# Dense attention's quotients stored, its finish loaded by chunks and joined with the norm, and idle matmuls at the head of eight stages

## The reference

```python
xn = _layernorm(x, ln_gamma, ln_beta)
q = (xn @ w_q).reshape(B, SQ, NUM_HEADS, DIM_HEAD)        # 16 heads of 64
k, v = jnp.split(context @ w_kv, 2, axis=-1)              # 1601 keys
attn = softmax(einsum('bqhd,bkhd->bhqk', q * SCALE, k))
out = einsum('bhqk,bkhd->bqhd', attn, v).reshape(B, SQ, INNER)   # INNER = 1024
return (out @ w_out + b_out) * tanh(gate[0])
...
x = _layernorm(x + _L1_xattn_ref(x, ...))
x = _layernorm(x + _L1_ffn_ref(x, ...))
```

## Time and profile before

| | us |
|---|---|
| median of three executions (lowest, highest) | 8678.82 (8678.73, 8685.87) |
| the profiled execution, whole | 8695.39 |
| the profiled execution, span of the trace | 8693.6 |
| busy in the span: PE, DVE, ACT, POOL | 6502.8, 6476.1, 4444.7, 3965.1 |
| dense attention `l1xc`, from the window's row | 6933 to 8447 |
| its finish and the norm behind it | 8447 to 8622 |

### The profile page before, as it was taken

One profiled execution on the slowest core, in us unless ns is written; L12 is line 12 of the kernel. 1 busy time (PEld: TensorE's weight loads), 2 busy tenths in 40 slices (PEclk: granted clock), 3 DMA queues, 4 the chain that ended last, 5 costly groups with the idle time before them and its releaser, 6 DMA issues. The chain is left out here.

```text
span 8693.6 us, 157925 instructions
## 1 busy us (share of the span) xinstructions
PE 6502.8 (75%) x31114; PEld 2666.4 (31%) x31240; DVE 6476.1 (74%) x41675; ACT 4444.7 (51%) x8491; POOL 3965.1 (46%) x2643
## 2 busy tenths in 40 slices
PE   6998477774677767998566777776657899999974
PEld 3333222221222224665222232222223322222213
DVE  4664899999999994554799999999996444444424
ACT  1665466664666652112567777776655332323320
POOL 0001355553555541221456666665644065656650
PEclk7999666665666667999677777776767999999986
DMA  2000000000000000000000000000000411111122
GB/s 75 19 22 12 31 8 5 8 5 4 8 5 8 8 2 17 22 15 16 32 9 5 7 8 9 6 9 5 6 5 19 164 31 31 38 40 31 31 47 64
DMA packets 81575, 193.10 MB, mean 22 GB/s; under 512 B 23728, under 2 KB 38062, under 8 KB 77230
## 3 DMA queue, kind: packets, MB, share of 16 engines
q1 hardware_dynamic: 72366, 169.98, 7.0%
q10 hardware_dynamic: 8192, 12.59, 0.6%
HBM read 118.97 MB, written 62.76 MB: 21 GB/s over the span
## 5 line engine op out<-in xcount | busy, mean ns | idle before, releaser
L2152 DVE TENSOR_REDUCE l1xc_part_max<-l1xc_by_query 128x1 f32<-128x512 f32 (+1 forms) x1024 | 559.5, 571 | 753.3 <-PE l1xc_by_query L2011 731.4
L2110 ACT ACTIVATE l1xc_prob<-l1xc_less_max 128x512 f32<-128x512 f32 (+1 forms) x832 | 451.2, 594 | 1004.4 <-PE l1xc_less_max L2025 935.9
L582 PE MATMUL l1ac_by_query<-l1ac_k_stack,l1ac_q_stack 97*128 (+1 forms) x1024 | 423.0, 470 | 695.8 <-ACT keep_xT L677 364.2
L770 DVE MAX8 l1ac_cand<-l1ac_score 128x8 f32<-128x39 f32 (+1 forms) x6656 | 863.1, 192 | 31.8 <-ACT l1ac_score L677 17.0
L552 POOL TENSOR_SCALAR l1ac_lost<-l1ac_score,l1ac_tops 128x2048 bf16<-128x2048 f32 x128 | 696.0, 5437 | 411.4 <-DVE l1ac_tops L789 387.1
L582 PE MATMUL l0xc_by_query<-l0xc_k_stack,l0xc_q_stack 97*128 (+2 forms) x1024 | 375.1, 431 | 664.8 <-ACT keep_xT L677 448.7
L770 DVE MAX8 l1ac_cand<-keep_xT 128x8 f32<-128x39 f32 (+1 forms) x6656 | 863.0, 191 | 4.4
L1973 POOL TENSOR_TENSOR l1xc_total<-l1xc_total,l1xc_prob 128x2048 f32<-128x2048 f32 (+1 forms) x176 | 794.2, 4513 | 72.3 <-POOL l1xc_v_tile L1983 72.0
L770 DVE MAX8 l0xc_cand<-l0xc_score 128x8 f32<-128x31 f32 (+1 forms) x6656 | 800.9, 182 | 27.6 <-ACT l0xc_score L677 15.8
L552 POOL TENSOR_SCALAR l1ac_lost<-keep_xT,l1ac_tops 128x2048 bf16<-128x2048 f32 x128 | 696.3, 5440 | 244.4 <-DVE l1ac_tops L789 244.4
L770 DVE MAX8 l0xc_cand<-keep_xT 128x8 f32<-128x31 f32 (+1 forms) x6656 | 801.7, 182 | 4.4
(11 more groups left out here) (479 smaller groups left out, 14320.9 us busy)
## 6 DMA issues: line engine op xcount, KB each, us to landing
l1xc_k<-wide_k SPq DMA_DIRECT2D x32, 400.2 KB
moe_w<-in_L_ffn_mlp_w_dram SPq DMA_DIRECT2D x16, 512.0 KB, 4.2
wide_q<-l1xp_full SPq DMA_DIRECT2D x8, 1024.0 KB, 3.9
wide_q_parts<-l1xp_parts SPq DMA_DIRECT2D x16, 512.0 KB, 5.5
l1xc_q_hm<-wide_q_parts SPq DMA_DIRECT2D x32, 256.0 KB, 3.8
l1xc_q<-wide_q SPq DMA_DIRECT2D x32, 256.0 KB
wide_sums<-l1xc_o_out ACTq DMA_DIRECT2D x64, 128.0 KB, 2.3
l1xf_num<-wide_sums SPq DMA_DIRECT2D x16, 512.0 KB, 11.6
```

The source lines that it names most:

```text
L582: nc.tensor.matmul(sA[c % 2][:, 0:w], Qm[0:SHIFT_ROW, bass.ds(at + i * P, P)], Kb[0:SHIFT_ROW, bass.ds(at + a, w)], start=True, stop=True) ...
L770: seg = nc.vector.max(new[:, j:8 * NSEG:NSEG], score[i % 4][:, a:a + w])
L2110: nc.scalar.activation(prob[0:n, buf(j), c], yP[c % 2][0:n], ACT.Exp).then_inc(y_taken, 1)
L2152: nc.vector.tensor_reduce(part_max[:, i % 2, c:c + 1], a_bank(i, c)[:, 0:w], AX.X, ALU.max).then_inc(a_taken, 1)
```

## The change

Six things are edited.

1. **Quotients are stored.** `denominators` runs in two halves, p = 0 at the end of tile j = 0 and p = 1 at the end of j = 1, each of two matmuls with ones of 64 columns; the second waits until DVE has emptied the bank. DVE takes two reciprocals (128x512 each) into a new tile `inv`, at the start of j = 1 and of j = 2. POOL multiplies `o_out` by them (`divide`, at the end of its j = 2 and j = 3). ACT's `store` moves from j = 2 to j = 4 and issues four DMAs where it issued eight.
2. **The finish's loads begin early.** SP loads `w_out` into the free `ctxT`, and the rows of the first four heads into `xT`, at the end of `attend_wide`. The other six chunks are loaded in `finish_wide` by groups of 512 queries (three DMAs of 512 KB each), with a semaphore for each group.
3. **No wait for all eight.** PE begins with a group's four tiles once its three loads have landed. DVE's eight multiplies are gone. The bias is added to x by POOL, times tanh(gate), as `finish_rows` does, so PE's matmul for it is gone.
4. **The norm is joined.** Statistics, roots and scalings follow tile by tile inside `finish_wide`, as in `finish_rows`; the block `l1xm` is gone. The transposes into `xT` stay.
5. **Idle matmuls** (`idle`, the same as L918): 14 ahead of each `project`, 20 ahead of each `layer_norm` but the last, 24 ahead of the gate's loads and 30 behind its logits, 28 ahead of `finish_wide`.
6. `wide_sums` has the shape (1024, 2048).

```diff
+def idle(nc, G, bank, n):
+    for _ in range(n):
+        nc.tensor.matmul(bank[:], G.identb[:], G.zerob[:], start=True, stop=True)
...
         @block.tensor                                   # project
         def _(pe):
+            idle(nc, G, banks[3], 14)
             pe.wait_ge(loaded, 6 * 16)
...
         @block.tensor                                   # layer_norm
         def _(pe):
+            if out is None:
+                idle(nc, G, banks[1], 20)
             if affine:
 
                 pe.wait_ge(loaded, 32)
...
         @block.tensor                                   # moe_gate
         def _(pe):
+            idle(nc, G, banks[2], 24)
             pe.wait_ge(loaded, LOADS)
...
             mm.then_inc(logged, 1)
+            idle(nc, G, banks[2], 30)
             pe.wait_ge(weighed, 1)
...
             stats(H - 1)                                # attend_wide, SP
+            w_out = G.ctxT[:].rearrange("p c n -> p (c n)")[:, 0:XC * D]
+            sp.dma_start(w_out.rearrange("p (c n) -> p c n", c=XC),
+                         A["L1_xattn_w_out"].rearrange("(c p) n -> p c n", p=P)).then_inc(fetched, 16)
+            sp.wait_ge(o_stored, 64 * 2 * KC + 16)
+            for c in range(KC):
+                sp.dma_start(G.xT[:, c], G.wide_sums[c * P:(c + 1) * P, :]).then_inc(fetched, 16)
+            sp.wait_ge(fetched, 16 * (KC + 1))
...
-                    hold(pool, (o_formed, h + 1))
+                    hold(pool, (o_formed, 2 * h + 2))
...
+            def divide(h, p):
+
+                hold(pool, (inverted, 2 * h + 3 + p), (o_taken, 2 * h + 4))
+                nc.gpsimd.tensor_tensor(O_out[:, p], O_out[:, p], inv[:, p], ALU.mult).then_inc(o_ready, 1)
...
-                for c in range(QC):
-                    mm = nc.tensor.matmul(Den[32 * c:32 * (c + 1), :], G.ones[:, 0:32], total[:, c],
+                hold(pe, (inverted, 2 * h + 2 + p))
+                if p == 0:
+                    hold(pe, (added_p, ADDS * (h + 2)), (st_out, h + 2 if last else h + 3))
+                for r in range(2):
+                    mm = nc.tensor.matmul(Den[r * XH:(r + 1) * XH, :], G.ones[:, 0:XH], total[:, 2 * p + r],
                                           start=True, stop=True, skip_group_check=True)
...
         @block.tensor                                   # finish_wide
         def _(pe):
-            pe.wait_ge(normed, XC)
+            def out(t):
+                if t % 4 == 0:
+                    pe.wait_ge(loaded[t // 4], 16 * EARLY // 2)
...
+            idle(nc, G, banks[3], 28)
+            pe.wait_ge(row_loaded, 32)
...
+            for t in range(QT):
+                out(t)
+                if t >= 6 and t % 4 == 2:
+                    turn_back(t // 4 - 1)
+            turn_back(G4 - 1)
```

More of the change, by code:

```diff
@@ L915, in turn_back @@
                     mm.then_inc(back_turned, 1)
-            for _ in range(IDLE):
-                nc.tensor.matmul(banks[3][:], G.identb[:], G.zerob[:], start=True, stop=True)
+            idle(nc, G, banks[3], 14)
             weights()
@@ L1995, in _ @@
             add(H - 1, NKT - 1)
+            for p in range(2):
+                divide(H - 1, p)
         @block.tensor
@@ L2074, in head @@
                             by_query(ha, 1 - slot, i, c)
-                    if j == 0 and not first:
-                        denominators(hb - 1)
+                    if j < 2 and not first:
+                        denominators(hb - 1, j)
             def a_end(h):
@@ L2238, in _ @@
-            nc.tensor.matmul(gate_bank[:, 0:1], G.ones[0:1, 0:P], gate[:], start=True, stop=True).then_inc(gated, 1)
-            pe.wait_ge(normed, XC)
-            for t in range(QT):
+            def out(t):
+                if t % 4 == 0:
+                    pe.wait_ge(loaded[t // 4], 16 * EARLY // 2)
                 if t >= 4:
@@ L2248, in _ @@
+            idle(nc, G, banks[3], 28)
+            pe.wait_ge(row_loaded, 32)
+            nc.tensor.matmul(row_bank[:, 0:D], G.ones[0:1, 0:P], bias[:], start=True, stop=True)
+            nc.tensor.matmul(row_bank[:, D:D + 1], G.ones[0:1, 0:P], gate[:], start=True, stop=True).then_inc(spread_formed, 1)
+            for t in range(QT):
+                out(t)
+                if t >= 6 and t % 4 == 2:
+                    turn_back(t // 4 - 1)
+            turn_back(G4 - 1)
         @block.scalar
```

158 lines of the change are left out of this document (100 added, 58 removed).

## The result

| us | before | after |
|---|---|---|
| median of the first comparison | 8682.35 (4 executions) | 8585.59 (4) |
| the traced execution | 8695.39 | 8583.69 |
| median of all executions of this study | 8685.7 (44; 8674.6 to 8708.3) | 8583.7 (8; 8571.5 to 8586.7) |

The ratio of the first comparison is 0.9886, 95% interval 0.9869 to 0.9903: faster by 1.1%. The forecast was 8554, range 8532 to 8577. So the direction was right and the forecast gain too large: 124.8 us forecast, 111.7 between the two traced executions, 102 between the medians of all.

The account below looks back on a forecast made before the run. Loads bound the finish's first part, PE its second, a DVE-ACT-DVE-PE chain its third; PE's waits count in the attention. -94.5 - 21 - 9.3 = -124.8, taken from the median 8678.82, gives 8554 us, range 8532 to 8577.

Parts of the forecast that it names:

- The finish: Final block of the dense attention: early loads and joined norm bring the next block 94.5 us earlier.
- The last quotients: Between attention and finish: two halves of sums, two reciprocals, a multiply and four issues end the block 2.8 us later.
- The load rate of 205 GB/s: Finish's first loads: 1.5 MB at the old rate take 7.3 us, so PE may start 9.3 us in.
- The attention: Dense attention: removing PE's waits on ACT saves 15.8 us over 14 heads and 5.2 in head 15, together 21.
- PE's four matmuls for `den` stay four.: Sums over the keys in each head: splitting them in two halves keeps four matmuls; reciprocals item taken as 0 us.
- The forecast's rival at 8575: Dense attention: a bank wait behind the reciprocals, 1.1 us a head, gives back the 21 us; chance 11%.
- The clock at the jumps: Loop jumps in the dense attention: clock falls, 20.6 us before, change by 0 in the middle, 12 either way.
- The stages are the same in the median run: Whole kernel: the gain against the traced 8695.39 us was also subtracted from the median 8678.82, giving 8554.
- The idle rows: Idle matmuls ahead of projections and norms and in the gate: gains and costs sum to -9.3 us.
- The gate: Idle matmuls there delay the chain by 3.2 to 4.2 us and save 1.5: net +2.2, bounds 0 and +4.
- the idle rows give nothing: Rival for the idle matmuls: 11.5 us of gains go, 3.7 of cost stay, about 8566; chance 14%.
- the list of what would show it: Trace signs named beforehand for right or wrong: waits on ACT, multiply times, first tile, tile spacing, gate's square, head lengths.

Follow-up runs that it names:

- e1: The kernel before the change, run once more unchanged: 8685.8 us, ratio 0.9994; its traced execution took 8696.4.
- e8: The changed kernel run again unedited, on the same chip as some of its variants: 8581.0 us, ratio 0.9884; its traced execution took 8571.5.
- e2: The changed kernel with one pass of sums a head (four 32-column matmuls), both reciprocals kept, output not the reference's: 8555.9 us, ratio 0.9845.
- e3: The changed kernel without any idle matmuls except the finish's 28: 8582.6 us, ratio 0.9877.
- e11: The changed kernel without the finish's 28 idle matmuls: 8581.7 us, ratio 0.9881; finish block 73.9 us against 73.2.
- e12: The changed kernel with each of the finish's twelve loads cut into two halves of 64 partitions: 8581.4 us, ratio 0.9887; finish block 75.0 us.
- e4: The changed kernel without the 24 idle matmuls at the head of the gate: 8577.4 us, ratio 0.9869; gate 71.7 us.
- e10: The changed kernel without the gate's 24 idle matmuls, and with 22 instead of 14 ahead of `l1ap`: 8581.3 us, ratio 0.9886; `l1ap` 80.6 us.
- e6: The changed kernel with four heads in one turn of the dense attention's loop, two jumps back instead of six: 8564.2 us, ratio 0.986.
- e7: The changed kernel with each of a head's four store DMAs cut into two of 32 rows, eight issues: 8582.7 us, ratio 0.9884.

## Why the prediction was wrong, step by step

The forecast was 29.7 us under the changed kernel's 8583.7 (the median of all its executions, and its first traced one). Of these 13.1 are terms of the sum, 9.7 the traced execution that the sum was made against (8695.4 over a median of 8685.7), and 6.9 the base: three executions gave 8678.8 where 44 give 8685.7. The 13.1 are good to some 13 us, since the traces of e1 and e8 differ by the full 124.9; so the steps below rest on stages and heads, and on e2 and e3, rather than on that sum.

- **The finish: right**, -96.9 for -94.5 (with e8's trace -94.5). The last quotients cost 2.0 more, 1.4 of it by the same step that failed in the attention: half of the sums was priced at half the time. The prediction's own sum is also some 0.4 short there: with its five hand-overs its terms end at 8451.0, not 8450.6. The block was 4.3 shorter: tiles 3.45 and not 3.65, since without the matmul of the bias between two tiles the eight take 0.2 less (3.2 in all), the start 0.4 and the tail 0.6 earlier. The load rate of 205 GB/s was wrong (388), but the idle row held the start: it ended 8.2 us in, and without it PE waited for the loads until 7.7 (e11). At 233 GB/s it would have been worth a wait of 1.0 (e12).
- **The attention: the failing step is "PE's four matmuls for `den` stay four."** Their time was taken as a time per instruction. It is a time per pass over the array's columns: four times 32 and twice 64 both take 1.06 to 1.08. e2 takes the second pass away and nothing else: PE's busy time in a head falls from 89.59 to 88.67 us and the head from 91.6 to 90.7. Rebuilt without chance: waits on ACT -15.8, last head -5.3 (72.6 to 67.3; -5.2 forecast), second pass +14, so -7 and not -21. The measured -18.6 holds 7.1 us of fewer clock falls (13.7 against 20.8) and some 4 us from the six heads with a jump, which gained 0.8 each where the others gained 0.1; why these gained more stays open. Over the eight traces with two passes a head this stretch is 1533.5 us on average, 13.7 under the kernel before. The forecast's rival at 8575 had the gain of the attention given back, which is the way it went, but by the wrong mechanism: a wait behind the reciprocals. Reciprocals and multiplies cost nothing (e2). "TensorEngine Tiling (Array Packing)" of the Trainium skill, section "Overview", gives up to four times the speed where one dimension is at most 32 and up to twice at 64. The traces agree with the factor of two between them, four products of 32 columns in 1.06 and two of 64 in 1.08; read beside the earlier trace rows (eight records, two to a matmul, with 32 columns in 1.93 at the lower clock) the section would have given the doubled cost.
- **The clock at the jumps: right as a spread, missed as a base.** 0 with 12 either way was -7.1; over the eight traces the falls are 12 to 24 us, 18 on average, against 21 in both traces of the kernel before. They can be a part of why executions of one kernel wander by 15 us, and not the whole: e8's traced execution was 12 us shorter than the first with a longer attention. "The stages are the same in the median run" was the step that failed here: nothing showed that it was so.
- **The idle rows: wrong.** -9.3 forecast, -1.4 measured, nothing in the medians (e3). They stand in seven stages, twice in the gate. `l0xp` -3.8 (forecast -3) and `l1ap` -3.1 (-4.5) are real, but the second hangs on a wait of 1.7 us (e4, e10). `l0ap`: none to be told from chance (-2.5). The norms: -0.2 (-1.5). The gate: +7.1 (+2.2), and +5.5 in the traces with 77.5, both outside its bounds. Its delay was nearly right (4.4); what failed was counting only the delay: the transposes and the logits lost 1.9 us of upper clock and the last products 1.1. The forecast's rival "the idle rows give nothing" (14%) describes this part, at 8566, and alone would still have missed.

Against the list of what would show it: no wait on ACT over 0.5 us and multiplies of 1.27, both right; the first tile 8.9 us in (9 to 10 said) and the square 4.4 later (3 to 4 said), both just outside; tiles and block shorter than said; heads without a jump of 91.6, where over 91 was named as the sign of a wrong step, and was one.

## What to carry to other kernels

Price a matmul by its share of the array's columns, not by its count: splitting one pass of four narrow products into two passes of wider ones doubled it here. An idle row paid only where the real work followed it with a short wait (up to 1.68 us here) and no small operation that releases another engine stood behind it. And a gain read between traces is to be taken from the trace's own time, with several executions of the kernel before to say where its median lies.

## What the runs showed of the hardware

- A `den` of four 128x32 products took 1.06 us, of two 128x64 products 1.08.
- Loads of 512 KB over 128 partitions ran at 388 GB/s, of 256 KB over 64 partitions at 233.
- Behind 2.97 us of idle matmuls at the upper clock, waits of PE of 1.45 to 1.68 us left it there in seven traces, and 1.71, 2.10 and 2.27 were followed by the lower clock. In the gate it fell while PE formed products of 8 columns without a pause (0.61 us a group, then 1.02).
- 24 idle matmuls ahead of the gate's small transposes made that stage 5.8 to 7.4 us longer (e4's 71.7 us, 77.5 and 79.1 with them); 28 ahead of the finish gave no gain that can be told (e11).
- A jump back of the loop left PE idle for 1.6 to 2.3 us; behind most of them the clock then fell, for 1.5 to 9 us of longer heads. Two jumps in place of six gained 17 us (e6).
- An issue on ACT of a 64x512 DMA took 0.64 us. One of 32x512 took 0.64 in the kernel before and 0.46 in e7; why they differ is open.
